# Graph attention, two layers: the last norm of a row block taken in smaller lots, and the last sweep closed tile by tile

## Chip, cores and metric
One core of one Trainium2 chip runs the whole program. The metric is the device time of an execution in microseconds (us); lower is better.

## What is computed
Two layers of graph attention over N = 4096 nodes with 256 features, each followed by a residual and a layer norm. Cut to what matters:

```python
# layer 1; layer 0 is alike with 8 heads of 128, an elu and a projection
xt  = einsum('ni,hio->hno', x, W)                 # 4 heads of 64
e   = leaky_relu(src[:, :, None] + dst[:, None, :], 0.2)
e   = where(adj > 0, e, -inf)
h   = einsum('hij,hjf->hif', softmax(e, axis=2), xt)
x   = layernorm(x + h.transpose(1, 0, 2).reshape(n, 256))
```

## The kernel before
Layer 0 takes the first 2255 us. Nothing in it is touched, except that two semaphores of GpSimd and SyncE become one.

Layer 1 runs in 16 sweeps `g`: four row blocks of 1024 rows, and in each the four heads. A sweep multiplies a 4096 x 1024 pattern by the head's values. The exponential of a sum is a product of exponentials on either side of the slope's kink, so the pattern is only zeros and ones, in two halves (`m` = 0 and 1), and the values come as high and low parts. A sweep has eight chunks `k` of 512 source rows. For a chunk ScalarE (and VectorE, for one of four rows of tiles in five of the eight chunks) compares thresholds (`compare2`, L1028 and L1422); VectorE masks the result with the adjacency and splits it (`split2`, L1433 and L1434); TensorE takes 64 matmuls (8 output tiles `t`, 4 source tiles, 2 halves) into eight PSUM banks, one for each output tile (`sweep2`, L835). Pattern buffers are four deep.

VectorE's order is written by hand. In sweep `g` it does the split of chunks 2 to 7 of `g` and of chunks 0 and 1 of `g + 1` (turns `m` = 0 to 7, L1577), each after the next turn's compare, and then takes the sums of `g` out of PSUM (`evacuate2`, L1443; ScalarE copies the first half, `copy_sums2`, L1042) and divides (`divide2`, L1451 to L1458, the last of them adds into `z`). So TensorE works on chunks 0 and 1 of the next sweep during that, and then waits for the split of chunk 2. TensorE may start a tile of the next sweep when VectorE has taken that tile's sums (`s_ev2`).

When the four heads of a row block are through, `z` holds x + h for its 1024 rows (eight tiles of 128 x 256). Its norm runs in the first sweep of the next block (g = 4, 8, 12): statistics of all eight tiles and their aggregation at turn 0 (`final_stats`, L1463, and `final_norm`, L1471 and L1473), a square root on ScalarE behind the compares of chunk 3 (`final_root`, L1046), a reciprocal at turn 2 (`final_scale`, L1478), and the scaling in two lots of four tiles at turns 3 and 4 (`final_apply`, L1483). SyncE's queue then stores `z` in one DMA, waits for it, and loads the next 1024 rows into it (L634, L636); the first head's `divide2` waits for that load (`s_zl`). Behind the last sweep the same steps run with nothing else left to do; there ScalarE scales four tiles (L1142) and VectorE the other four, and two DMAs store them (L651).

Of the kernel before, what the change touches and what calls it, by code (L numbers as in the profile page):

```python
# [17 lines left out]
P = 128  # L18
# [12 lines left out]
CPB = 8  # L31
# [56 lines left out]
def network(nc, x, adj, W, a1, a2, feat, W_out, b_out, Wn, c1, c2, x1, out):  # L88
# [28 lines left out]
    with ExitStack() as ctx:  # L117
# [64 lines left out]
        s_xm, s_pw, s_cw, s_mo = (s.sem(n) for n in ("xm", "pw", "cw", "mo"))  # L182
# [19 lines left out]
        CW2 = blk2 // 4  # L202
        G2, FIRST, WHOLE = H2 * NB2, H2, CPB - 2
# [54 lines left out]
        s_tn, s_rr, s_oh, s_ol = (s.sem(n) for n in ("tn", "rr", "oh", "ol"))  # L258
# [8 lines left out]
        s_zl, s_sd, s_sq, s_rs2, s_ap, s_o = (s.sem(n) for n in ("zl", "sd", "sq", "rs_", "ap", "o"))  # L267
        s_fin = [s.sem(f"fin_{p}") for p in range(2)]
# [77 lines left out]
        def _(pool):  # L346
# [45 lines left out]
            def ones2(c):  # L392
                pool.wait_ge(s_f2, c + 1)
                if c > 0:
                    pool.wait_ge(s_us, 16 * c)
                if c == CPB - 1:
                    pool.wait_ge(s_uv2[0][WHOLE], 16)
                nc.gpsimd.tensor_copy(stage_one(0), by_head(eu2, c))
                nc.gpsimd.tensor_copy(stage_one(2), by_head(ev2, c)).then_inc(s_oh, 1)
                pool.wait_ge(s_oh, c + 1)  # L400
                nc.gpsimd.tensor_tensor(stage_one(1), by_head(eu2, c), stage_one(0), ALU.subtract)
                nc.gpsimd.tensor_tensor(stage_one(3), by_head(ev2, c), stage_one(2), ALU.subtract).then_inc(s_ol, 1)
# [21 lines left out]
        def _(sp):  # L424
# [64 lines left out]
            def store_stage(c):  # L489
# [4 lines left out]
                sp.wait_ge(s_ol, c + 1)  # L494
# [13 lines left out]
            def tiles(dram, b):  # L508
                return dram.rearrange("(t p) f -> p t f", p=P)[:, b * TPB2:(b + 1) * TPB2, :]
# [107 lines left out]
            sp.dma_start(z[:, :, :], tiles(x1, 0)).then_inc(s_zl, 16)  # L617
# [31 lines left out]
            for p in range(2):  # L649
                sp.wait_ge(s_fin[p], 1)  # L650
                sp.dma_start(tiles(out, NB2 - 1)[:, p * TPB2 // 2:(p + 1) * TPB2 // 2, :],  # L651
                             z[:, p * TPB2 // 2:(p + 1) * TPB2 // 2, :]).then_inc(s_o, 16)
            sp.wait_ge(s_o, 16 * (NB2 + 1))

        @block.tensor
        def _(pe):
# [152 lines left out]
            def sweep2(g):  # L809
# [3 lines left out]
                for k in range(CPB):  # L813
# [29 lines left out]
                    last.then_inc(s_pe2, 1)  # L843

# [53 lines left out]
        def _(act):  # L898
# [148 lines left out]

            for n in range(16):
                copy_x(n)
# [73 lines left out]
            for g in range(G2):  # L1123
                if g > 0:
                    compare2(g, ahead2, range(lead, JC2))
                for k in range(ahead2 + 1 if g > 0 else CPB - 1, CPB):
                    compare2(g, k, range(JC2))
                    if g > 0 and g % H2 == 0 and k == ahead2 + 1:
                        final_root(g // H2 - 1)
# [5 lines left out]
                copy_sums2(g, 0)  # L1135
                if g + 1 < G2:
                    compare2(g + 1, ahead2, range(lead))
                copy_sums2(g, batch)
            final_root(NB2 - 1)
            act.wait_ge(s_n, 2 * NT + 2 * NB2 + 1)  # L1140
            for u in range(TPB2 // 2, TPB2):
                ins = act.activation(z[:, u, :], z[:, u, :], ACT.Identity, bias=mv[:, u, 1:2], scale=rs[:, u:u + 1])  # L1142
            ins.then_inc(s_fin[1], 1)

        @block.vector
        def _(dve):
# [289 lines left out]
            def evacuate2(g):  # L1436

                for t in range(TPB2):
                    if g == 0 and t == 0:
                        dve.wait_ge(s_sx, 1)  # L1440
                    if t % batch == 0:
                        dve.wait_ge(s_e2, TPB2 // batch * g + (t // batch + 1))
# [3 lines left out]
            def divide2(g):  # L1446

                h, b = g % H2, g // H2
                dve.wait_ge(s_ev2, TPB2 * (g + 1))
                ch = Chain(dve, s_dv2, 3 * g)  # L1450
                ch.link(dve.tensor_tensor(vt2, vt2, e2[:, :, V1:2 * V1], ALU.add))  # L1451
                ch.link(dve.reciprocal(zr2[:, :], vt2[:, :, D2:V1].rearrange("p t a -> p (t a)")))
                v = vt2[:, :, 0:D2]
                ch.link(dve.tensor_tensor(v, v, zr2[:, :].unsqueeze(2).to_broadcast([P, TPB2, D2]), ALU.mult))  # L1454
                if h == 0:
                    dve.wait_ge(s_zl, 16 * (b + 1))
                part = z[:, :, h * D2:(h + 1) * D2]
                dve.tensor_tensor(part, part, v, ALU.add).then_inc(s_dz, 1)  # L1458

            def final_stats(b, tiles):  # L1460
                dve.wait_ge(s_dz, H2 * (b + 1))
                for u in tiles:
                    last = dve.bn_stats(st[:, u, :], z[:, u, :])  # L1463
                last.then_inc(s_n, 1)

            def final_norm(b):
                at = 2 * NT + 2 * b
                dve.wait_ge(s_n, at + 1)
                ch = Chain(dve, s_n, at + 1)
                for u in range(TPB2):  # L1470
                    last = dve.bn_aggr(mv[:, u, :], st[:, u, :])  # L1471
                ch.link(last)
                dve.tensor_scalar(rt[:, :], mv[:, :, 1:2].rearrange("p u a -> p (u a)"), LN_EPS, None,  # L1473
                                  ALU.add).then_inc(s_sd, 1)

            def final_scale(b):
                dve.wait_ge(s_sq, b + 1)
                dve.reciprocal(rs[:, :], rt[:, :]).then_inc(s_rs2, 1)  # L1478

            def final_apply(b, tiles, signal):  # L1480
                dve.wait_ge(s_rs2, b + 1)
                for u in tiles:
                    last = dve.tensor_scalar(z[:, u, :], z[:, u, :], mv[:, u, 0:1], rs[:, u:u + 1], ALU.subtract,  # L1483
                                             ALU.mult)
                last.then_inc(signal, 1)
# [89 lines left out]
            for g in range(G2):  # L1575
                turns = [(g, k) for k in range(ahead2, CPB)] + ([(g + 1, k) for k in range(ahead2)] if g + 1 < G2 else [])
                for m, (gk, k) in enumerate(turns):  # L1577
# [30 lines left out]
                evacuate2(g)  # L1608
                divide2(g)
# [5 lines left out]
            final_stats(NB2 - 1, range(TPB2))  # L1615
            final_norm(NB2 - 1)
            final_scale(NB2 - 1)
            dve.wait_ge(s_rs2, NB2)
            dve.scalar_tensor_tensor(mv[:, :, 1:2].rearrange("p u a -> p (u a)"),
                                     mv[:, :, 0:1].rearrange("p u a -> p (u a)"), -1.0, rs[:, :],  # L1620
                                     ALU.mult, ALU.mult).then_inc(s_n, 1)
            final_apply(NB2 - 1, range(TPB2 // 2), s_fin[0])
# [26 lines left out]
```

## Time and profile before
| | |
|---|---|
| median of 3 runs | 2777.14 us (2777.05 to 2778.43) |
| the profiled execution | 2780.41 us, span 2778.7 us |
| TensorE busy | 2686.8 us, 97% |
| VectorE busy | 1982.1 us, 71% |
| ScalarE busy | 2064.3 us, 74% |
| granted TensorE clock | 0.991 on average |

Times in rows are microseconds from the start of the span. Engines: PE is TensorE, PEld its weight loads, DVE VectorE, ACT ScalarE, SPq the DMA queue that SyncE issues on. A row of a timeline has start, length, engine, line, operation, what it writes and reads, and how many instructions were merged; in brackets stands how long the engine was idle before it and what ended that.

### The profile page before, as it was taken

Reading aid. Unit: us, or ns where it says so; the run is one execution under the profiler, and the core shown is the slowest. Engines: PE = TensorE matmul, PEld = TensorE weight load, DVE = VectorE, ACT = ScalarE, POOL = GpSimd, SP = SyncE. Lnnn points to the kernel's source line nnn. Section 1 sums busy time; section 2 is a strip of 40 time slices with the busy share of each in tenths; the row PEclk is TensorE's granted clock in tenths of the full one; section 3 lists DMA queues with packets and bytes.
Section 4 is the critical chain, followed back from the end, with each engine's and each line's share of the span. In section 5 each row is a group of like instructions: output and inputs, shape, how many; then the busy total and the mean of one; then the engine's idle time right before and its main releaser. Section 6 shows DMA issues by size and latency. Waiting matters only on the chain.

```text
span 2778.7 us, 62377 instructions
## 1 busy us (share of the span) xinstructions
PE 2686.8 (97%) x26475; PEld 2327.5 (84%) x26475; DVE 1982.1 (71%) x3186; ACT 2064.3 (74%) x3216; POOL 563.7 (20%) x449
## 2 busy tenths in 40 slices
PE   7879999999999999999999999999999989999997
PEld 3438887888888888888888888888888879999997
DVE  5455669667776776777677677675655679988897
ACT  4447787677777777777777777777764579999996
POOL 0030018223231422323232142230002310000000
PEclk9999999999999999999999999999999999999999
DMA  7995431110110101111010111002115555323330
GB/s 248 392 328 178 152 114 45 30 34 22 42 30 23 40 26 30 37 31 30 20 43 27 27 37 34 26 21 56 34 46 166 185 194 190 109 79 121 105 109 17
DMA packets 192793, 241.57 MB, mean 87 GB/s; under 512 B 14074, under 2 KB 113658, under 8 KB 192508
## 3 DMA queue, kind: packets, MB, share of 16 engines
q1 hardware_dynamic: 192516, 237.59, 26.5%
q8 instruction: 209, 3.42, 0.5%
q14 instruction: 68, 0.56, 0.1%
HBM read 179.69 MB, written 57.05 MB: 85 GB/s over the span
## 4 chain that ended last, share of the span: by engine, by line
PE 73%; DVE 5%; ACT 4%; issue 1%; POOL 0%; DMA 0%; ACTq 0%; DVEq 0%
PE l_ps L726 57%; PE l_ps L835 9%; PE l_ps L763 4%; ACT l_arena L1028 3%; PE l_ps L788 1%; DVE l_arena L1434 1%; PE l_ps L751 1%; DVE l_arena L1433 1%; DVE l_arena L1443 1%; ACT l_arena L1042 0%; DVE l_arena L1463 0%; DVE l_arena L1422 0%; DVE l_arena L1451 0%; DVE l_arena L1454 0%; DVE l_arena L1458 0%
## 5 line engine op out<-in xcount | busy, mean ns | idle before, releaser
L726 PE MATMUL l_ps<-l_arena 128*128 128x258 f16 x16384 | 1834.8, 273 | 6.3 <-POOL l_arena L380 3.4
L726 PEld LDWEIGHTS l_ps<-l_arena 128*128 128x128 fp8e4 x16384 | 1592.8, 97 | 246.0 <-issue 3.7
L941 ACT ACTIVATE l_arena<-l_arena 128x512 fp8e4<-128x512 f32 x2048 | 1281.4, 708 | 89.2 <-PE l_ps L726 89.1
L1240 DVE SCALAR_TENSOR_TENSOR l_arena<-l_arena,l_mask 128x512 uint32<-128x512 uint32 x512 | 469.2, 916 | 408.4 <-ACT l_arena L941 405.6
L835 PE MATMUL l_ps<-l_arena 128*128 128x130 f16 x8192 | 487.6, 221 | 23.2 <-DVE l_arena L1434 13.3
L835 PEld LDWEIGHTS l_ps<-l_arena 128*128 128x128 fp8e4 x8192 | 482.5, 98 | 28.2 <-DVE l_arena L1434 22.9
L1241 DVE TENSOR_TENSOR l_arena<-l_arena,l_mask 128x512 uint32<-128x512 uint32 x512 | 490.2, 957 | 0.0
L1028 ACT ACTIVATE l_arena<-l_arena 128x1024 fp8e4<-128x1024 f32 x434 | 456.7, 1142 | 3.5 <-PE l_ps L835 3.4
L373 POOL TENSOR_TENSOR l_arena<-l_arena 128x516 f32<-128x516 f32 x120 | 156.8, 1306 | 1264.1 <-PE l_ps L726 1172.3
L959 ACT COPY l_arena<-l_ps 128x258 f32<-128x258 f32 x256 | 93.5, 368 | 245.2 <-PE l_ps L726 245.2
L1246 DVE SCALAR_TENSOR_TENSOR l_arena<-l_ps,l_arena 128x258 f32<-128x258 f32 x256 | 117.0, 482 | 147.9 <-ACT l_arena L959 147.9
L380 POOL TENSOR_TENSOR l_arena<-l_arena 128x516 f16<-128x516 f32 x120 | 176.5, 1488 | 32.5 <-DVE l_arena L1227 28.1
L1433 DVE SCALAR_TENSOR_TENSOR l_arena<-l_arena,l_mask 128x1024 uint32<-128x1024 uint32 x128 | 156.4, 1222 | 28.7 <-ACT l_arena L1028 27.8
L374 POOL TENSOR_TENSOR l_arena<-l_arena 128x516 f16<-128x516 f32 x120 | 174.4, 1453 | 0.0
L1434 DVE TENSOR_TENSOR l_arena<-l_arena,l_mask 128x1024 uint32<-128x1024 uint32 x128 | 156.1, 1219 | 0.0
L693 PE MATMUL l_ps<-l_mask 128*128 128x512 f32 x264 | 131.2, 637 | 0.0
L947 ACT ACTIVATE l_arena<-l_arena 128x512 f32<-128x512 f32 x64 | 40.6, 635 | 109.3 <-DVE l_arena L1272 109.3
L763 PE MATMUL l_ps<-l_arena 128*128 128x256 f32 x512 | 116.6, 381 | 0.0
L763 PEld LDWEIGHTS l_ps<-l_arena 128*128 128x128 f32 x512 | 95.8, 190 | 14.0 <-ACT l_arena L965 0.2
L913 ACT COPY l_arena<-l_ps 128x512 f32<-128x512 f32 x66 | 38.3, 582 | 90.6 <-DMA l_wh<-l_arena 67.5
L1202 DVE TENSOR_SCALAR l_arena<-l_arena 128x1024 fp8e4<-128x1024 int32 x52 | 40.0, 769 | 76.1 <-ACT l_arena L925 76.0
L693 PEld LDWEIGHTS l_ps<-l_mask 128*128 128x128 f32 x264 | 50.2, 203 | 48.7 <-issue 48.4
(152 smaller groups left out, 1208.8 us busy)
## 6 DMA issues: line engine op xcount, KB each, us to landing
l_arena<-in_adj SPq DMA_DIRECT2D x128, 512.0 KB, 6.5
l_arena<-uv SPq DMA_DIRECT2D x125, 260.0 KB, 5.7
l_wh<-l_arena SPq DMA_DIRECT2D x64, 256.0 KB, 9.5
l_arena<-l_srow SPq DMA_DIRECT2D x64, 256.0 KB, 3.2
l_arena<-l_wh SPq DMA_DIRECT2D x64, 256.0 KB, 4.7
feat<-l_arena SPq DMA_DIRECT2D x64, 256.0 KB, 2.2
l_arena<-feat SPq DMA_DIRECT2D x32, 512.0 KB, 3.6
uv<-l_arena SPq DMA_DIRECT2D x8, 1040.0 KB, 5.1
```

The source lines that it names most:

```text
L374: last = nc.gpsimd.tensor_tensor(part(h, c, j), whx[k][:, :, :], factor(f, h, c), ALU.mult)
L380: last = nc.gpsimd.tensor_tensor(part(h, c, j + 1), t[:, :, :], part(h, c, j), ALU.subtract)
L693: last = nc.tensor.matmul(banks[i % 3], rowsof, wall[:, k, q * H // 2:(q + 1) * H // 2, :], start=(k == 0), stop=(k == KF - 1))
L726: last = nc.tensor.matmul(sums(t, m), pattern(k, m).bitcast(F8)[:, j, t * P:(t + 1) * P], uv[:, slot(h, order[k]) + j, 2 * m * W1:2 * (m + ...
L763: last = nc.tensor.matmul(py[t % 2], ft[t % 2][:, k, :], wo[:, k, :], start=(k == 0), stop=(k == KO - 1))
L835: last = nc.tensor.matmul(sums2(t, m), pattern2(k, m).bitcast(F8)[:, j, t * P:(t + 1) * P], uv2[:, q, at:at + 2 * V1], start=(k == 0 and j ...
L941: ins = act.activation(pattern(k, 0).bitcast(F8)[:, j, :], s1b[q][:, :], ACT.Relu, bias=kc[:, h, jt:jt + 1], scale=STEEP, saturate=False)
L1028: ins = act.activation(pattern2(k, 0).bitcast(F8)[:, j, :], s1b2[:, q, :], ACT.Relu, bias=kc2[:, g % H2, jt:jt + 1], scale=STEEP, saturate ...
L1240: dve.scalar_tensor_tensor(c, v, ONE8X4, m, ALU.bitwise_xor, ALU.bitwise_and)
L1241: dve.tensor_tensor(v, v, m, ALU.bitwise_and).then_inc(s_bc, 1)
L1433: dve.scalar_tensor_tensor(c, v, ONE8X4, m, ALU.bitwise_xor, ALU.bitwise_and)
L1434: dve.tensor_tensor(v, v, m, ALU.bitwise_and).then_inc(s_bc2, 1)
```

## The change
- At a block's end (g = 4, 8, 12): statistics of tiles 0 to 3 at turn 0, of tiles 4 to 7 and the aggregation at turn 1; ScalarE's root after the compares of chunk 6 instead of chunk 3; the reciprocal at turn 4; scaling of tiles 0 to 2, 3 to 5, 6 and 7 at turns 4, 5 and 6.
- SyncE stores `z` and loads its next rows in three parts (`parts2`: tiles 0 to 2, 3 to 5, 6 and 7), each load after the store of the same part, in place of one DMA each way. The first load of `z` is three DMAs too.
- In the last sweep TensorE does chunks 0 to 4 as before, then waits for all patterns of the last three chunks and goes through them tile by tile (`CLOSE` is 3), so that a tile's sums are complete every 24 matmuls.
- Behind it everything goes in four pairs of tiles: ScalarE copies a pair's sums, VectorE evacuates, divides and takes the pair's statistics, ScalarE takes the root, VectorE makes the factors (`last_shift`), ScalarE alone scales, and SyncE stores 256 KB.
- `evacuate2` waits before each tile instead of before each fourth.

```diff
@@ SyncE, block end
-                    sp.wait_ge(s_ap, 2 * (g // H2))
-                    sp.dma_start(tiles(out, g // H2 - 1), z[:, :, :]).then_inc(s_o, 16)
-                    sp.wait_ge(s_o, 16 * (g // H2))
-                    sp.dma_start(z[:, :, :], tiles(x1, g // H2)).then_inc(s_zl, 16)
+                    b = g // H2 - 1
+                    for p, (first, last) in enumerate(parts2):
+                        sp.wait_ge(s_ap, 3 * b + p + 1)
+                        sp.dma_start(tiles(out, b, first, last), z[:, first:last, :]).then_inc(s_o[p], 16)
+                        if p > 0:
+                            sp.wait_ge(s_o[p - 1], 16 * (b + 1))
+                            load_z(b + 1, *parts2[p - 1])
+                    sp.wait_ge(s_o[2], 16 * (b + 1))
+                    load_z(b + 1, *parts2[2])
@@ TensorE, last sweep
-                for k in range(CPB):
+                for k in range(CPB - CLOSE if g == G2 - 1 else CPB):
...
+                if g == G2 - 1:
+                    pe.wait_ge(s_bc2, CPB * G2)
+                    for t in range(TPB2):
+                        for k in range(CPB - CLOSE, CPB):
+                            for j in range(JC2):
+                                ...
+                        if t < TPB2 - 1:
+                            last.then_inc(s_mm2, 1)
+                    last.then_inc(s_pe2, CLOSE)
@@ ScalarE
-                    if g > 0 and g % H2 == 0 and k == ahead2 + 1:
+                    if g > 0 and g % H2 == 0 and k == CPB - 2:
                         final_root(g // H2 - 1)
...
+            last_sums(0)
+            last_sums(1)
+            for p in range(4):
+                last_root(p)
+                if p < 2:
+                    last_sums(p + 2)
+                last_apply(p)
@@ VectorE, block end
-                        if m == 0:
-                            final_stats(g // H2 - 1, range(TPB2))
-                            final_norm(g // H2 - 1)
-                        if m == 2:
-                            final_scale(g // H2 - 1)
-                        if m in (3, 4):
-                            final_apply(g // H2 - 1, range(4 * (m - 3), 4 * (m - 2)), s_ap)
+                        if m < 2:
+                            final_stats(HALF * m, HALF * (m + 1), g)
+                        if m == 1:
+                            final_norm(0, TPB2, 2 * NT + 3 * b + 2)
+                        if m == 4:
+                            final_scale(0, TPB2, b + 1)
+                        if 4 <= m < 7:
+                            final_apply(b, *parts2[m - 4])
@@ VectorE, behind the last sweep
+            for p, (first, last) in enumerate(pairs2):
+                evacuate2(G2 - 1, first, last, lambda t: TPB2 // batch * (G2 - 1) + t // 2 + 1)
+                divide2(G2 - 1, first, last, 3 * (G2 - 1 + p))
+                if p > 0:
+                    last_shift(p - 1)
+                final_stats(first, last, G2 + p)
+                final_norm(first, last, base + 3 * p + 1)
+            last_shift(len(pairs2) - 1)
```

## Rows read from the trace of the kernel before
**Rows 1.** The page, part 4: the chain that ended last, by line of code.
```profile
PE l_ps L726 57%; PE l_ps L835 9%; PE l_ps L763 4%; ACT l_arena L1028 3%; PE l_ps L788 1%; DVE l_arena L1434 1%; PE l_ps L751 1%; DVE l_arena L1433 1%; DVE l_arena L1443 1%; ACT l_arena L1042 0%; DVE l_arena L1463 0%; DVE l_arena L1422 0%; DVE l_arena L1451 0%; DVE l_arena L1454 0%; DVE l_arena L1458 0%
```

**Rows 2.** Timeline of TensorE, last sweeps: start, length, instructions, idle before, releaser.
```profile
2518.91 3.91 PE L835 MATMUL l_ps<-l_arena 128*128 128x130 f16 x64 [0.36 <-DVE l_arena L1434]
2525.33 20.21 PE L835 MATMUL l_ps<-l_arena 128*128 128x130 f16 x320 [2.52 <-DVE l_arena L1434]
2546.26 37.66 PE L835 MATMUL l_ps<-l_arena 128*128 128x130 f16 x640 [0.71 <-DVE l_arena L1443]
2584.28 30.20 PE L835 MATMUL l_ps<-l_arena 128*128 128x130 f16 x512 [0.36 <-DVE l_arena L1434]
...
2672.74 37.64 PE L835 MATMUL l_ps<-l_arena 128*128 128x130 f16 x640 [2.07 <-DVE l_arena L1443]
...
2741.30 22.59 PE L835 MATMUL l_ps<-l_arena 128*128 128x130 f16 x384 [0.36 <-DVE l_arena L1434]
```

**Rows 3.** Timeline of VectorE and ScalarE in the ninth sweep, same columns.
```profile
2518.76 2.71 DVE L1463 BATCH_NORM_STATS2 l_arena<-l_arena 128x6 f32<-128x256 f32 x8
...
2522.38 0.21 ACT L1046 ACTIVATE l_arena<-l_arena 128x8 f32<-128x8 f32 x1 [4.86 <-DVE l_arena L1473]
2522.50 20.88 ACT L1028 ACTIVATE l_arena<-l_arena 128x1024 fp8e4<-128x1024 f32 x20
...
2525.81 1.23 DVE L1433 SCALAR_TENSOR_TENSOR l_arena<-l_arena,l_mask 128x1024 uint32<-128x1024 uint32 x1 [0.54 <-ACT l_arena L1028]
2526.96 1.22 DVE L1434 TENSOR_TENSOR l_arena<-l_arena,l_mask 128x1024 uint32<-128x1024 uint32 x1
...
2529.90 1.22 DVE L1433 SCALAR_TENSOR_TENSOR l_arena<-l_arena,l_mask 128x1024 uint32<-128x1024 uint32 x1 [1.00 <-ACT l_arena L1028]
...
2543.49 1.23 DVE L1433 SCALAR_TENSOR_TENSOR l_arena<-l_arena,l_mask 128x1024 uint32<-128x1024 uint32 x1 [0.50 <-ACT l_arena L1028]
...
2545.76 2.33 DVE L1443 SCALAR_TENSOR_TENSOR l_arena<-l_ps,l_arena 128x130 f32<-128x130 f32 x8
```

**Rows 4.** DMA issues of the whole run: count, KB each, median us to landing.
```profile
l_arena<-uv SPq DMA_DIRECT2D x125, 260.0 KB, 5.7
...
l_arena<-in_x SPq DMA_DIRECT2D x32, 128.0 KB, 2.3
x<-l_arena SPq DMA_DIRECT2D x32, 128.0 KB, 1.7
l_arena<-x SPq DMA_DIRECT2D x4, 1024.0 KB, 5.5
out<-l_arena SPq DMA_DIRECT2D x3, 1024.0 KB, 4.9
```

**Rows 5.** Two stretches by window; PEclk is the granted TensorE clock.
```profile
2525.30:2528.00 2.70, 2.67 (x25) 2.67 (x26) 2.19 (x2) 2.70 (x4) 0.00 (x0) 0.50 0.00 0
...
2651.80:2656.00 4.20, 4.20 (x72) 4.20 (x73) 3.09 (x4) 4.20 (x5) 0.00 (x0) 1.00 0.01 4
```

**Rows 6.** Timeline of the last 25 us, columns as in rows 2.
```profile
2754.68 1.22 DVE L1434 TENSOR_TENSOR l_arena<-l_arena,l_mask 128x1024 uint32<-128x1024 uint32 x1
...
2763.99 0.59 ACT L1042 COPY l_arena<-l_ps 128x520 f32<-128x520 f32 x1 [1.27 <-PE l_ps L835]
...
2772.51 2.07 ACT L1142 ACTIVATE l_arena<-l_arena 128x256 f32<-128x256 f32 x4 [0.47 <-DVE l_arena L1619]
2773.79 1.20 SPq L651 DMA_DIRECT2D out<-l_arena  x2
```

**Rows 7.** Groups of layer 1 by line and shape: busy us, mean ns.
```profile
L1422 DVE TENSOR_SCALAR l_arena<-l_arena 128x1024 fp8e4<-128x1024 f32 x78 | 60.0, 770 | 8.9 <-PE l_ps L835 8.9
...
L1451 DVE TENSOR_TENSOR l_arena<-l_arena 128x520 f32<-128x520 f32 x16 | 11.2, 700 | 0.5
...
L1046 ACT ACT_TABLE_LOAD x1 | 1.3, 1283 | 0.0
...
L1381 DVE TENSOR_TENSOR l_arena<-l_arena 128x24 f32<-128x24 f32 x1 | 0.2, 182 | 0.0
```

More of the change, by code:

```diff
@@ L506, in store_rows, with tiles, load_z @@
                     sp.dma_start(srow2[:, at:at + P], rows2[c % 2][t * H2:(t + 1) * H2, :]).then_inc(s_ro2[c % 2], 16)
-            def tiles(dram, b):
-                return dram.rearrange("(t p) f -> p t f", p=P)[:, b * TPB2:(b + 1) * TPB2, :]
+            def tiles(dram, b, first, last):
+                return dram.rearrange("(t p) f -> p t f", p=P)[:, b * TPB2 + first:b * TPB2 + last, :]
+            def load_z(b, first, last):
+                sp.dma_start(z[:, first:last, :], tiles(x1, b, first, last)).then_inc(s_zl, 16)
             def load_next():
@@ L616, in _ @@
             sp.wait_ge(s_xp, NT)
-            sp.dma_start(z[:, :, :], tiles(x1, 0)).then_inc(s_zl, 16)
+            for first, last in parts2:
+                load_z(0, first, last)
             store_rows(CPB - 2)
@@ L648, in _ @@
                             store_back(g + 1, n if g % 2 else WHOLE - 1 - n)
[L649 to L653, printed above, removed]
+            for p, (first, last) in enumerate(pairs2):
+                sp.wait_ge(s_fin, p + 1)
+                sp.dma_start(tiles(out, NB2 - 1, first, last), z[:, first:last, :]).then_inc(s_o[0], 16)
+            sp.wait_ge(s_o[0], 16 * (NB2 - 1 + len(pairs2)))
         @block.tensor
@@ L1443, in evacuate2, with divide2 @@
                     dve.scalar_tensor_tensor(e2[:, t, :], sums2(t, 1), sc2[:, g % H2, g // H2 * TPB2 + t:g // H2 * TPB2 + t + 1],
                                              e2[:, t, :], ALU.mult, ALU.add).then_inc(s_ev2, 1)
-            def divide2(g):
+            def divide2(g, first, last, base):
                 h, b = g % H2, g // H2
[L1449 to L1454, printed above, removed]
-                if h == 0:
-                    dve.wait_ge(s_zl, 16 * (b + 1))
-                part = z[:, :, h * D2:(h + 1) * D2]
-                dve.tensor_tensor(part, part, v, ALU.add).then_inc(s_dz, 1)
@@ L1460, in final_stats @@
[L1460 to L1473, printed above, removed]
+                dve.wait_ge(s_ev2, TPB2 * g + last)
@@ new lines, in divide2 @@
+                ch = Chain(dve, s_dv2, base)
+                part = vt2[:, first:last, :]
+                inverse = zr2[:, first:last]
+                ch.link(dve.tensor_tensor(part, part, e2[:, first:last, V1:2 * V1], ALU.add))
+                ch.link(dve.reciprocal(inverse, part[:, :, D2:V1].rearrange("p t a -> p (t a)")))
+                v = part[:, :, 0:D2]
+                ch.link(dve.tensor_tensor(v, v, inverse.unsqueeze(2).to_broadcast([P, last - first, D2]), ALU.mult))
+                if h == 0:
+                    dve.wait_ge(s_zl, 48 * (b + 1))
@@ new lines, in divide2, with final_stats, final_norm @@
+                into = z[:, first:last, h * D2:(h + 1) * D2]
+                dve.tensor_tensor(into, into, v, ALU.add).then_inc(s_dz, 1)
+            def final_stats(first, last, ready):
+                dve.wait_ge(s_dz, ready)
+                for u in range(first, last):
+                    ins = dve.bn_stats(st[:, u, :], z[:, u, :])
+                ins.then_inc(s_n, 1)
+            def final_norm(first, last, base):
+                dve.wait_ge(s_n, base)
+                ch = Chain(dve, s_n, base)
+                for u in range(first, last):
+                    ins = dve.bn_aggr(mv[:, u, :], st[:, u, :])
+                ch.link(ins)
+                dve.tensor_scalar(rt[:, first:last], mv[:, first:last, 1:2].rearrange("p u a -> p (u a)"), LN_EPS, None,
@@ L1474, in final_norm, with final_scale, final_apply @@
                                   ALU.add).then_inc(s_sd, 1)
[L1476 to L1480, printed above, removed]
+            def final_scale(first, last, count):
+                dve.wait_ge(s_sq, count)
+                dve.reciprocal(rs[:, first:last], rt[:, first:last]).then_inc(s_rs2, 1)
+            def final_apply(b, first, last):
                 dve.wait_ge(s_rs2, b + 1)
[L1482 to L1485, printed above, removed]
+                for u in range(first, last):
+                    ins = dve.tensor_scalar(z[:, u, :], z[:, u, :], mv[:, u, 0:1], rs[:, u:u + 1], ALU.subtract, ALU.mult)
+                ins.then_inc(s_ap, 1)
```

83 lines of the change are left out of this document (55 added, 28 removed).

## Prediction

> **What bounds the kernel.** I read the page's chain first. TensorE holds most of it, and layer 1's matmuls (L835) are 9% of the span [rows 1]. So a microsecond counts only where TensorE waits, or behind its last matmul. The timeline of TensorE alone shows where that is. In a plain sweep 512 matmuls take 30.20 us and 0.36 us is idle, so from one start of chunk 2 to the next are 30.56 us [rows 2]. Around a block's end it is different: from 2518.91 to 2584.28, two sweeps, are 65.37 us against 61.12, so a block's end costs 4.25 us. The trace has three, each with a wait of 2.51 or 2.52 us before chunk 3 and another before the next sweep (0.71 in the one shown, 2.07 in the last [rows 2]).
>
> The timeline of VectorE and ScalarE says who causes it. VectorE's statistics sit between the split of chunk 2 and of chunk 3; ScalarE stands at its root for 4.86 us until they are through; and since its compares are then late, VectorE itself idles 0.54, 1.00 and 0.50 us before three later splits [rows 3]. TensorE's next sweep starts 0.50 us after VectorE begins to take the sums (2545.76 to 2546.26 [rows 2, 3]). So VectorE's row of work, and not TensorE's 30 us, sets the length of this sweep.
>
> Last I read the end of the timeline. Three chunks at 3.75 us (37.66 us hold ten and 0.16 of pipeline [rows 2]) after 2741.30 end chunk 4 at 2752.6. The last split ends at 2755.9. TensorE ends at 2763.89; 14.8 us follow.
>
> **Block's end, added up.** Zero is 2518.76, the start of the statistics. Costs from start to start: an instruction behind another starts 0.08 to 0.09 us before the end of the one ahead (1.23 long, 1.15 apart), so a split is 2.27 [rows 3], a compare, 0.77 long [rows 7], takes 0.66 to 0.68, and a statistic 0.33 (2.71 for eight [rows 3]).
> - Turn 0: four statistics 1.31, compare 0.66, split of chunk 3 2.27: 4.24. TensorE needs 0.14 from a split's end to its start; it starts chunk 3 at 4.38 instead of 3.90, a wait near 0.5.
> - Turn 1: four statistics with their wait 1.43, aggregation and epsilon. The old row of eight statistics to epsilon takes 3.50, from 2518.76 to 2522.26, of which 2.74 are statistics; 0.76 is left. The split of chunk 4 ends at 8.70; TensorE wanted it at 8.13, a second wait of 0.7.
> - Turns 2 to 4: two compares, two splits 14.56; reciprocal with its wait 0.24; three tiles at 0.32 (four L1483 take 1.29) 15.77.
> - Turns 5 to 7: three splits, one compare, five tiles: 24.86.
>
> Before, the same mark, the first L1443, lies at 27.00. The three idles from start to start come to 2.25 (2.04 shown, and some 0.07 of lost overlap at each); 27.00 - 2.25 + 0.11 for the second lot's and the factor's waits gives 24.86 again. Does a new idle come in? ScalarE's compares are 1.044 apart (20 in 20.88 [rows 3]). Without the stop at the root it has chunk 4 at 1.9, 5 at 6.0, 6 at 9.2, 7 at 12.4, the next sweep's 0 and 1 at 17.0 and 20.1; VectorE wants them at 6.4, 9.4, 12.3, 15.8, 19.7 and 22.6. The least room is 2.5 us. The table load before the first root, 1.28 once [rows 7] and so far hidden behind ScalarE's stop, fits. TensorE has finished the sweep at 23.8 and starts the next at 25.36 instead of 27.50. From there all is as before. **Gain 2.14 us at each of three ends: 6.4 us.** The cost of work isn't less; what goes are idles. Bounds: 0 if other idles take their place, 2.25 if the second lot's wait is free.
>
> **Reload of z.** The last scaling ends at 22.7 instead of 19.0, the add needs `z` at 28.9. From 128 KB in 1.7 and 1024 KB in 4.9 a store is 3.6 ns for a KB and 1.25 fixed; loads (2.3 and 5.5) are 1.85 fixed [rows 4]. The last part, 256 KB, is stored by 24.9 and loaded by 27.7; the longer parts went before. Room 1.2 us, so I take 0. The issues behind it on SyncE's queue (a row load and eight of the values) start some 1.5 us later and are wanted 30 us later. The first load as three DMAs delays that queue by two issues, 0.8 us, at the start of layer 1; Taken as 0, at most 0.8.
>
> **Per-tile waits.** Three more waits a sweep lie on the path. Eight evacuations take 2.33 us with a wait in the middle that ended late [rows 3]; waits already met have no row of their own. Between 0 and 0.03 us each (the gap that a true chain shows): 0 to 1.4 us over 15 sweeps. I take 0, since the wait can be read while the 0.35 us instruction ahead runs.
>
> **The close.** TensorE now needs the last split before the first of three chunks. It ends at 2755.8 [rows 6], so matmuls start at 2755.95 instead of 2752.6: 3.3 us late, for sure. A pair of tiles is 48 matmuls, 2.82 us.
> VectorE's pair: evacuation 0.66; add of 130 columns, reciprocal, product, add into `z`. Their price I take on the line between 24 columns in 0.182 and 520 in 0.700 [rows 7], 1.04 ns a column: 0.29 each, the reciprocal 0.17, with waits 1.13. Then the factors of the pair ahead 0.29, two statistics 0.77, aggregation 0.29, epsilon 0.08: **3.2 us**, against TensorE's 2.82. So VectorE sets the pace from the first pair on. Its first pair starts 3.48 after TensorE's start (2.98 and 0.1, as at 2763.99 [rows 6], and the copy of 260 columns, 0.4), at 2759.43; the fourth's epsilon ends 12.7 later, at 2772.1. ScalarE's root and the factors are 0.70, two tiles of scaling 1.08 (four take 2.07 [rows 6]): 2773.9. A 256 KB store lands in 2.2 and 0.4 closes the span: 2776.5. Against 2778.7 that is a gain of 2.2 us.
>
> **The clock.** After one wait of 2.52 us the granted clock was 0.50, the 1.2 GHz level; after another of 2.51 it was 1.00, 2.4 GHz [rows 5]. At 0.50 the 320 matmuls took 20.21 us instead of 18.9, 1.3 more; it cost nothing, as VectorE was later still. TensorE's wait before the close is 3.2 us and has nothing behind which to hide: each pair comes 1.3 later. I take the fall as likelier than not: **gain of the close 0.9 us** with it, 2.2 without.
> The Trainium skill, "TensorE: Matmul & The Clock Gate", section "Why this matters for your kernels", tells kernels to avoid gaps between bursts because the clock then falls back to its lower level. By that rule the sum is the 0.9; the trace agrees in some of its waits only.
>
> **Sum.** 6.4 + 0.9 = 7.3 us, made on the profiled span; 2780.41 of that execution lies 3.3 above the median, which shifts the level and not the difference. 2777.14 - 7.3 = **2769.8 us**.
>
> **Rivals.**
> - *Full clock in the close* (0.25): 2777.14 - 6.4 - 2.2 = 2768.5. For it: one of the three long waits at block ends left the clock up [rows 5].
> - *The block ends give only part* (0.17). The clock may now fall at the start of sweeps 5, 9 and 13, after a wait of 1.5 us, where TensorE has no room: up to 3 x 1.3 = 3.9 us, 2773.7. Against it: 640 matmuls after the wait of 2.07 took 37.64, no more than the 37.66 after 0.71 [rows 2]. Or idles of VectorE return by half: 3.2, 2773.0.
> - *The pairs don't pay* (0.10). Many short instructions for few: if a pair costs VectorE 3.7 instead of 3.2 (each small step 0.05 dearer), the end is 2.0 later and the close loses 1.1: 2771.8.
> - *Slower* (0.03). The reload of z comes late: four transfers share one queue at the same time. Transfers of 260 KB had a median of 5.7 us [rows 4]. If store and load of the last part each took that, `z` would be there at 34.1, 5.2 late, of which 0.25 is room: 3 x 4.9 = 14.8, 2784.6. It decides from a landing at 31.6. Against it: that median is of queues of eight; here one part waits for another's store.
>
> **How the numbers follow.** The forecast has 0.45. A measurement here can tell about 0.2%, 5.6 us, from no change. Below 2771.6 lie the forecast, the first rival and a bit of the others: faster 0.73; the rest of the partial cases: same 0.24; slower 0.03. Range 2767.2 (full clock, a pair of 3.0, 0.4 more at the end) to 2773.8 (next to all of the partial cases).
>
> **What the new profile must show.** Waits of 0.5 and 0.7 before chunks 3 and 4 in place of 2.5, and about 1.5 before sweeps 5, 9 and 13; two sweeps at a block's end in 63.2 us; VectorE never idle on ScalarE there, ScalarE no longer at the root; a wait of 3.2 before the close and perhaps a clock of 0.50; pairs 3.2 apart on VectorE; some 2.5 us from the last issue to the end. Wrong it would be if L1458's successor waited for a DMA, or if sweeps 5, 9, 13 ran at the lower clock.

## The result and the profile after

| | before | changed |
|---|---|---|
| median | 2777.97 us (17 runs) | 2771.68 us (17 runs) |
| ratio | | 0.9975, 95% interval 0.9969 to 0.9982 |
| profiled execution, span | 2778.7 us | 2769.8 us |

The kernel became 0.25% faster, 6.3 us by the medians; 7.3 were forecast. The two profiled spans differ by 8.9 us, more than that, and the trace says where. Layer 0, where only two semaphores became one, was 3.7 us shorter in this execution (layer 1's first matmul is at 2251.61 and was at 2255.35), and sweeps 0 to 3 were 1.4 longer. About 1.0 of the 1.4 is sweep 1, whose 512 matmuls took 31.25 us instead of 30.21; the granted clock was 0.50 in its first 2.7 us. What the change touches is 5.3 us at the block ends and 1.3 us in the close: 5.3 + 1.3 + 3.7 - 1.4 = 8.9. So I compare stretches of the profiled executions, one for each run, and not spans: two sweeps from the start of chunk 2 at a block's end to the start of chunk 2 two sweeps on, and the last sweep's chunk 2 to the end of the span.

TensorE's timeline in the changed kernel, with the same columns as [rows 2]. L846 are the sweeps, L865 is the close:

```profile
2514.43 3.91 PE L846 MATMUL l_ps<-l_arena 128*128 128x130 f16 x64 [0.36 <-DVE l_arena L1485]
2518.66 3.91 PE L846 MATMUL l_ps<-l_arena 128*128 128x130 f16 x64 [0.33 <-DVE l_arena L1485]
2523.13 15.12 PE L846 MATMUL l_ps<-l_arena 128*128 128x130 f16 x256 [0.56 <-DVE l_arena L1485]
2539.65 37.92 PE L846 MATMUL l_ps<-l_arena 128*128 128x130 f16 x640 [1.39 <-DVE l_arena L1493]
2577.93 30.20 PE L846 MATMUL l_ps<-l_arena 128*128 128x130 f16 x512 [0.37 <-DVE l_arena L1485]
...
2664.26 7.64 PE L846 MATMUL l_ps<-l_arena 128*128 128x130 f16 x128 [1.40 <-DVE l_arena L1493]
2672.55 30.19 PE L846 MATMUL l_ps<-l_arena 128*128 128x130 f16 x512 [0.66 <-DVE l_arena L1485]
...
2733.66 11.38 PE L846 MATMUL l_ps<-l_arena 128*128 128x130 f16 x192 [0.36 <-DVE l_arena L1485]
2748.32 12.64 PE L865 MATMUL l_ps<-l_arena 128*128 128x130 f16 x192 [3.28 <-DVE l_arena L1485]
```

At the ninth sweep the wait of 2.52 us is gone. In its place are 0.33, 0.56 and, before the next sweep, 1.39 (0.48, 0.72 and 1.52 more than a plain chunk, from start to start). The two sweeps from 2514.43 to 2577.93 take 63.50 us; before they took 65.37 [rows 2]. The three block ends take 63.23, 63.50 and 64.07. The last is the dearest, and one more wait shows in it, 0.66 us in front of chunk 2 at 2672.55.

VectorE, ScalarE and SyncE's queue in the same sweep (L1515 statistics, L1075 root, L1493 evacuation, L1510 the add into `z`, L643 and L515 store and load of `z`, L479 and L485 loads of rows and values):

```profile
2514.29 1.40 DVE L1515 BATCH_NORM_STATS2 l_arena<-l_arena 128x6 f32<-128x256 f32 x4
...
2518.53 1.40 DVE L1515 BATCH_NORM_STATS2 l_arena<-l_arena 128x6 f32<-128x256 f32 x4
...
2523.34 0.20 ACT L1075 ACTIVATE l_arena<-l_arena 128x8 f32<-128x8 f32 x1
...
2536.99 0.37 SPq L643 DMA_DIRECT2D out<-l_arena  x1
2537.41 2.18 SPq L515 DMA_DIRECT2D l_arena<-x  x2
...
2539.16 2.16 DVE L1493 SCALAR_TENSOR_TENSOR l_arena<-l_ps,l_arena 128x130 f32<-128x130 f32 x8
...
2539.69 0.41 SPq L479 DMA_DIRECT2D l_arena<-srow  x1
2540.14 5.49 SPq L485 DMA_DIRECT2D l_arena<-uv  x8
...
2543.69 0.69 DVE L1510 TENSOR_TENSOR l_arena<-l_arena 128x512 f32<-128x512 f32 x1 [0.67 <-DMA l_arena<-x]
```

The root no longer has an idle ahead of it (4.86 us in [rows 3]). From the first statistic to the first evacuation are 2539.16 - 2514.29 = 24.87 us, where it was 27.00. The last row is new: VectorE waits 0.67 us for the load of `z`. In the last block end the same wait is 1.24 us.

The close: copies of a pair's sums on ScalarE, the first evacuation of each pair on VectorE, the last scaling on ScalarE:

```profile
2752.65 0.38 ACT L1083 COPY l_arena<-l_ps 128x260 f32<-128x260 f32 x1 [6.85 <-PE l_ps L865]
2753.06 0.61 DVE L1493 SCALAR_TENSOR_TENSOR l_arena<-l_ps,l_arena 128x130 f32<-128x130 f32 x2 [4.79 <-ACT l_arena L1083]
...
2756.04 0.60 DVE L1493 SCALAR_TENSOR_TENSOR l_arena<-l_ps,l_arena 128x130 f32<-128x130 f32 x2
...
2759.15 0.61 DVE L1493 SCALAR_TENSOR_TENSOR l_arena<-l_ps,l_arena 128x130 f32<-128x130 f32 x2
...
2762.27 0.61 DVE L1493 SCALAR_TENSOR_TENSOR l_arena<-l_ps,l_arena 128x130 f32<-128x130 f32 x2
...
2766.14 1.09 ACT L1093 ACTIVATE l_arena<-l_arena 128x256 f32<-128x256 f32 x2 [0.43 <-DVE l_arena L1541]
```

The evacuations start 2.98, 3.11 and 3.12 us apart. TensorE's matmuls started at 2748.32 behind a wait of 3.28 us. In windows at its start (PEclk is the third number from the right):

```profile
2748.30:2751.00 2.70, 2.68 (x25) 2.68 (x26) 0.00 (x0) 0.00 (x0) 0.00 (x0) 0.50 0.00 0
2751.00:2755.00 4.00, 4.00 (x70) 4.00 (x69) 1.77 (x7) 0.38 (x1) 0.00 (x0) 0.99 0.02 4
```

The clock was granted at 0.50, the 1.2 GHz level, for the first 2.7 us, with 25 matmuls in them; after that 70 fit into 4.0 us. The 192 take 12.64 us and not 11.4.

### The profile page after: what moved, and what is told of

Same layout as the page of the kernel before. It is cut to its first block, busy times and chain, and to the rows that moved or that the text cites. A ratio compares the mean times of both kernels' runs of the same rounds, so it can differ in the third digit from the quotient of the medians.

```text
span 2769.8 us, 62417 instructions
## 1 busy us (share of the span) xinstructions
PE 2681.0 (97%) x26475; PEld 2322.7 (84%) x26475; DVE 1982.7 (72%) x3203; ACT 2068.0 (75%) x3225; POOL 563.8 (20%) x449
## 4 chain that ended last, share of the span: by engine, by line
PE 73%; DVE 6%; ACT 2%; issue 1%; DMA 0%; POOL 0%; ACTq 0%; DVEq 0%
PE l_ps L737 57%; PE l_ps L846 9%; PE l_ps L774 4%; ACT l_arena L1057 2%; DVE l_arena L1485 1%; DVE l_arena L1484 1%; PE l_ps L799 1%; PE l_ps L762 1%; DVE l_arena L1473 1%; DVE l_arena L1493 1%; ACT l_arena L1071 0%; DVE l_arena L1515 0%; DVE l_arena L1510 0%; DMA l_arena<-x 0%; DVE l_arena L1503 0%
## 5 line engine op out<-in xcount | busy, mean ns | idle before, releaser
L846 PE MATMUL l_ps<-l_arena 128*128 128x130 f16 x8000 | 476.1, 220 | 19.6 <-DVE l_arena L1485 9.5
L846 PEld LDWEIGHTS l_ps<-l_arena 128*128 128x128 fp8e4 x8000 | 470.3, 98 | 25.3 <-DVE l_arena L1485 20.7
```

The source lines that it names most:

```text
L846: last = nc.tensor.matmul(sums2(t, m), pattern2(k, m).bitcast(F8)[:, j, t * P:(t + 1) * P], uv2[:, q, at:at + 2 * V1], start=(k == 0 and j ...
```

## Experiments

All compare stretches as above; "ends" are the three pairs of sweeps and "close" is chunk 2 of the last sweep to the end. The kernel before has 65.37, 65.37, 65.37 and 37.4. A ratio is taken to runs of the kernel before on the same chip; their medians are 2778.01 (e1 to e4), 2779.11 (e5 to e8) and 2778.86 us (e9 to e12).

| run | ends, us | close, us | median, us | ratio to before, 95% |
|---|---|---|---|---|
| changed | 63.23, 63.50, 64.07 | 36.1 | 2771.68 | 0.9975 (0.9969 to 0.9982) |
| e1 close only | 65.38, 65.37, 65.36 | 36.5 | 2776.19 | 0.9994 (0.9986 to 1.0003) |
| e2 block ends only | 63.24, 63.42, 63.22 | 37.4 | 2771.34 | 0.9973 (0.9965 to 0.9982) |
| e3 statistics in one lot | 65.37, 65.29, 65.26 | 34.9 | 2775.06 | 0.9990 (0.9981 to 0.9999) |
| e4 root early | 68.30, 68.45, 68.29 | 36.1 | 2786.15 | 1.0029 (1.0018 to 1.0039) |
| e5 queue waits for z | 63.23, 63.24, 63.50 | 36.3 | 2768.48 | 0.9967 (0.9954 to 0.9979) |
| e6 scaling a turn earlier | 63.24, 63.24, 63.25 | 36.5 | 2768.88 | 0.9966 (0.9954 to 0.9978) |
| e7 close of two chunks | 63.24, 63.46, 64.06 | 34.3 | 2768.30 | 0.9964 (0.9951 to 0.9976) |
| e8 both | 63.24, 63.24, 63.24 | 34.2 | 2767.38 | 0.9958 (0.9946 to 0.9971) |
| e9 one transfer | 66.65, 68.41, 68.50 | 36.2 | 2784.59 | 1.0024 (1.0015 to 1.0033) |
| e10 close of one chunk | 63.23, 63.65, 63.72 | 37.0 | 2771.39 | 0.9974 (0.9965 to 0.9983) |
| e11 changed, again | 63.22, 63.51, 63.50 | 34.8 | 2772.57 | 0.9978 (0.9969 to 0.9987) |
| e12 both, again | 63.23, 63.22, 63.23 | 34.3 | 2768.54 | 0.9964 (0.9951 to 0.9978) |

Medians and stretches agree only roughly. For e5 the medians give 10.6 us and the stretches 7.2; for e11 they give 6.3 and 8.5. Only the profiled execution of each run has a trace; what the others did in layer 0, at the ends and in the close is not known.

### e1 and e2: each half of the change alone

e1 keeps the block ends of before (root behind chunk 3, reciprocal at turn 2, two lots of scaling, one DMA each way):

```diff
-                        if m < 2:
-                            final_stats(HALF * m, HALF * (m + 1), g)
-                        if m == 1:
+                        if m == 0:
+                            final_stats(0, HALF, g)
+                            final_stats(HALF, TPB2, g)
                             final_norm(...)
-                        if m == 4:
+                        if m == 2:
                             final_scale(...)
-                        if 4 <= m < 7:
-                            final_apply(b, *parts2[m - 4])
+                        if m in (3, 4):
+                            final_apply(b, 4 * (m - 3), 4 * (m - 2))
```

> Only the close of the last sweep is changed; at the three block ends statistics, root, scaling and the one store and load of z stand as before. Theory (two separate gains): two sweeps at a block end stay at 65.4 us; from the last sweep's chunk 2 to the end of the span 36.1 to 36.2 us against 37.4 before, with the clock at 0.50 at the close's start, so the kernel is 1.3 us faster than before. Rival (the close pays nothing, the changed kernel's gain is all from the block ends): 37.4 us again, no change in time.

e2 keeps the last sweep of before:

```diff
-                for k in range(CPB - CLOSE if g == G2 - 1 else CPB):
+                for k in range(CPB):
...
-            for p, (first, last) in enumerate(pairs2):
-                ...
+            final_stats(0, TPB2, G2)
+            final_norm(0, TPB2, base + 1)
+            final_scale(0, TPB2, NB2)
```

> Only the block ends are changed; the last sweep and what follows it are as before. Theory: two sweeps at the three ends take 63.2, 63.5 and 64.1 us (65.4 before), give or take 0.4 for the landing of z, so 5.3 us faster than before, and 37.4 us from the last chunk 2 to the end. Rival (the close brings more than its own 1.3 us, since the sweeps' clock or transfers act on each other): less than 4 us faster.

The two gains stand apart, as both theories had it, with two stretches off their numbers: e1's close is 36.5 us where 36.1 to 36.2 were expected, and e2's third end is 63.22 where 64.1 was. TensorE in e1 (L841 sweeps, L860 close):

```profile
2519.98 20.17 PE L841 MATMUL l_ps<-l_arena 128*128 128x130 f16 x320 [2.52 <-DVE l_arena L1480]
2540.91 37.65 PE L841 MATMUL l_ps<-l_arena 128*128 128x130 f16 x640 [0.76 <-DVE l_arena L1488]
...
2750.59 12.96 PE L860 MATMUL l_ps<-l_arena 128*128 128x130 f16 x192 [3.28 <-DVE l_arena L1480]
```

The wait of 2.52 at the block's end and the 3.28 before the close stand side by side. e1's close is 0.9 us shorter than before, and the interval of its ratio includes 1: by the times the close alone can't be told from nothing. e2 has 6.2 us less in its three ends (2.13 + 1.95 + 2.15) and is 0.27% faster. So what the measurement sees is the block ends.

### e3: statistics in one lot, root late

```diff
-                        if m < 2:
-                            final_stats(HALF * m, HALF * (m + 1), g)
-                        if m == 1:
+                        if m == 0:
+                            final_stats(0, HALF, g)
+                            final_stats(HALF, TPB2, g)
                             final_norm(...)
```

> The changed kernel with the statistics of all eight tiles at turn 0 again; the late root and the late scaling in three lots stay. Theory (what goes is VectorE's idling behind ScalarE's early root): TensorE waits 2.5 us before chunk 3 as in the kernel before, yet the first evacuation still starts 24.8 us after the statistics and two sweeps take 63.2 to 64.1 us; time that of the changed kernel. Rival (what goes is TensorE's wait of 2.5 us before chunk 3, by the two lots): two sweeps go back to 65.4 us, 5 to 6 us slower than the changed kernel.

My theory missed here, and the rival's number came out: 65.3 us. TensorE, and at the end of the ninth sweep ScalarE's copy of the sums:

```profile
2518.50 3.91 PE L846 MATMUL l_ps<-l_arena 128*128 128x130 f16 x64 [0.36 <-DVE l_arena L1485]
2524.92 27.96 PE L846 MATMUL l_ps<-l_arena 128*128 128x130 f16 x448 [2.51 <-DVE l_arena L1485]
2543.50 0.59 ACT L1071 COPY l_arena<-l_ps 128x520 f32<-128x520 f32 x1 [2.01 <-PE l_ps L846]
2553.24 30.19 PE L846 MATMUL l_ps<-l_arena 128*128 128x130 f16 x512 [0.36 <-DVE l_arena L1485]
2583.79 30.20 PE L846 MATMUL l_ps<-l_arena 128*128 128x130 f16 x512 [0.36 <-DVE l_arena L1485]
...
2740.71 11.38 PE L846 MATMUL l_ps<-l_arena 128*128 128x130 f16 x192 [0.36 <-DVE l_arena L1485]
2755.36 11.39 PE L865 MATMUL l_ps<-l_arena 128*128 128x130 f16 x192 [3.27 <-DVE l_arena L1485]
```

The 448 matmuls behind the wait take 27.96 us. At 3.75 us a chunk, and 0.16, they should take 26.4. The windows say what held them (and, second, that in this execution the clock did not fall in the close):

```profile
2524.90:2528.00 3.10, 3.08 (x29) 3.08 (x30) 3.10 (x4) 2.71 (x4) 0.00 (x0) 0.50 0.00 0
...
2755.30:2758.00 2.70, 2.64 (x46) 2.65 (x47) 0.00 (x1) 0.00 (x0) 0.00 (x0) 1.00 0.00 0
```

At all three ends the granted clock was 0.50 or 0.52 behind the wait. So there are two rows of work of about the same length at a block's end. VectorE's is 27.0 us to the first evacuation in the kernel before and 24.9 in the changed one. TensorE's is the wait of 2.5, its 30 us, and 1.5 us of lower clock. Before, the fall was hidden behind VectorE: the third end, where the clock stayed up [rows 5], took 65.37 as well. With the late root VectorE is out of the way (the copy waits 2.01 us for TensorE, and TensorE does not wait before the next sweep), and TensorE's own row sets 65.3. The late root alone buys 0.1 us in this execution. Without the fall it would be about 65.3 - 1.5 = 63.8 us an end, an estimate from these rows. The profiled execution, 2777.71 us, is among the slowest of e3's eleven (2771.07 to 2777.94), so in others the clock may have stayed up; no trace shows them.

### e4: statistics in two lots, root early

```diff
-                    if g > 0 and g % H2 == 0 and k == CPB - 2:
+                    if g > 0 and g % H2 == 0 and k == ahead2 + 1:
                         final_root(g // H2 - 1)
```

> The changed kernel with ScalarE's root behind the compares of chunk 3 again; the statistics stay in two lots. Theory: ScalarE stands some 7.7 us until the epsilon at turn 1, VectorE idles 3.3, 1.2 and 0.2 us behind it, the first evacuation starts 29.8 us after the statistics, two sweeps take 68 us, 8 us more than before over three ends, 12 to 14 us slower than the changed kernel. Rival (the two lots alone make the gain): 63.2 to 64.1 us, time of the changed kernel.

As the theory had it: VectorE waits for ScalarE's compares up to 3.5 us, and TensorE for VectorE.

```profile
DVE l_arena L1484 <- ACT l_arena L1057: 29.1, 36, 3.5
```

```profile
2525.49 3.91 PE L846 MATMUL l_ps<-l_arena 128*128 128x130 f16 x64 [0.33 <-DVE l_arena L1485]
2533.52 17.39 PE L846 MATMUL l_ps<-l_arena 128*128 128x130 f16 x256 [4.12 <-DVE l_arena L1485]
```

68.3 to 68.5 us at each end, 3 us more than before. The two lots with the early root are worse than nothing. Each half of the reordering needs the other: the lots keep TensorE's waits short, so that the clock stays up, the late root keeps ScalarE going, and together they give 2.1 us.

### e5 and e6: the late load of z

e5 holds the row load and the eight value loads back until `z` has landed:

```diff
+                if g > 0 and g % H2 == 0:
+                    sp.wait_ge(s_zl, 48 * (g // H2 + 1))
                 if g < G2 - 2:
                     sp.wait_ge(s_ca2, CPB * (g + 1))
```

> The changed kernel, but at a block end SyncE waits for all three loads of z before it issues the row load and the eight loads of the values. Theory (the last part of z lands late because those nine transfers share the 16 DMA engines with it): VectorE's wait for z (0.67 and 1.24 us in two of the changed kernel's three block ends) is gone, the last part lands 2.8 us after its issue instead of 4.5 to 5.0, and two sweeps take 63.2 to 63.3 us at all three. Rival (the last part is late by itself, behind its own store and the second part's load): waits of 0.5 to 1.2 us stay and one pair of sweeps is at 64 us again.

SyncE's queue in e5 at the ninth sweep (two loads of `z`, then the row load behind the wait), and VectorE's wait for `z` in all three ends:

```profile
2540.44 2.15 SPq L515 DMA_DIRECT2D l_arena<-x  x2
...
2545.28 0.33 SPq L479 DMA_DIRECT2D l_arena<-srow  x1
```

```profile
DVE l_arena L1512 <- DMA l_arena<-x: 0.7, 1, 0.7
```

The second load is issued near 2542.2 and the queue goes on at 2545.28, 3.1 us later; in the changed kernel the same load took 4.4. Two of the three ends are at 63.23 and 63.24. But one wait of 0.7 stayed: there the load took 4.4 us with nothing behind it in the queue. And the changed kernel's first end has the nine transfers right behind the load too, which landed soon all the same:

```profile
L515 SPq DMA_DIRECT2D l_arena<-x x1: 367/367/367, 2414.8 to 2414.8; - x1
DMA to landing us min/median/max: 3.1/3.1/3.1
```

Landings of the last part, in us, at the three ends:

| | first | second | third |
|---|---|---|---|
| changed, e2, e7, e10 and e11: nine behind | 3.1 to 3.9 | 4.3 to 4.6 | 4.1 to 5.0 |
| e5: none behind | 3.0 | 3.0 | 4.4 |
| e6, e8 and e12: nine behind, a turn earlier | 2.7 to 2.8 | 2.8 to 4.5 | 2.8 to 4.4 |

So the theory holds at the second end and the rival at the third. Nine transfers behind a load do not make it late by themselves, as its landings after 2.7 and 2.8 us in e6 show; what else does stays open.

The Trainium skill, "DMA: Bandwidth & Descriptors", section "Issuing engines are not separate DMA queues", says that transfers share the same 16 DMA engines and interleave. The second end agrees, with 3.0 us against 4.3 to 4.6; the third does not show it.

e6 makes `z` ready earlier, with the root behind chunk 5:

```diff
-                    if g > 0 and g % H2 == 0 and k == CPB - 2:
+                    if g > 0 and g % H2 == 0 and k == CPB - 3:
                         final_root(g // H2 - 1)
...
-                        if m == 4:
+                        if m == 3:
                             final_scale(0, TPB2, b + 1)
-                        if 4 <= m < 7:
-                            final_apply(b, *parts2[m - 4])
+                        if 3 <= m < 6:
+                            final_apply(b, *parts2[m - 3])
```

> The changed kernel with the root behind the compares of chunk 5 and the reciprocal and scaling one turn earlier (turns 3, 4, 5). Theory: VectorE's work is the same, so the first evacuation still starts 24.9 us after the statistics; the last scaling ends 2.9 us earlier, z is there in time, and two sweeps take 63.2 us at all three block ends, 1 us faster than the changed kernel. Rival (ScalarE's root now comes too near to the epsilon and ScalarE's compares are late again): VectorE idles behind ScalarE in these sweeps and they take 64 us or more.

```profile
2512.24 3.91 PE L846 MATMUL l_ps<-l_arena 128*128 128x130 f16 x64 [0.37 <-DVE l_arena L1485]
...
2575.48 30.20 PE L846 MATMUL l_ps<-l_arena 128*128 128x130 f16 x512 [0.36 <-DVE l_arena L1485]
...
2636.59 3.91 PE L846 MATMUL l_ps<-l_arena 128*128 128x130 f16 x64 [0.36 <-DVE l_arena L1485]
...
2699.84 30.20 PE L846 MATMUL l_ps<-l_arena 128*128 128x130 f16 x512 [0.36 <-DVE l_arena L1485]
```

2575.48 - 2512.24 and 2699.84 - 2636.59 are 63.24 and 63.25 us, and VectorE's waits for `z` are gone: even a load of 4.0 us is in time here, and in e8 one of 4.5. That is the number of the forecast for a block's end with nothing late.

### e7 and e10: how many chunks to close tile by tile

```diff
-        HALF, CLOSE = TPB2 // 2, 3
+        HALF, CLOSE = TPB2 // 2, 2        # e10: 1
```

> The changed kernel with CLOSE = 2: only the last two chunks are gone through tile by tile. Theory (the close with three chunks pays its gain back by a wait of 3.3 us for the last split and by the clock that falls in it): no wait before the close, clock at 1.00, VectorE's first pair starts 17.6 us after chunk 2's start instead of 19.4, from chunk 2 to the end 34.3 us instead of 36.1, 1.8 us faster than the changed kernel. Rival (the earlier first pair is of no use, since the last pair waits for TensorE or for ScalarE): 35.5 us or more.

TensorE in e7, then VectorE's first evacuation in e7 and in e10:

```profile
2736.03 15.12 PE L846 MATMUL l_ps<-l_arena 128*128 128x130 f16 x256 [0.36 <-DVE l_arena L1485]
2750.98 7.63 PE L865 MATMUL l_ps<-l_arena 128*128 128x130 f16 x128
```

```profile
2753.51 0.61 DVE L1493 SCALAR_TENSOR_TENSOR l_arena<-l_ps,l_arena 128x130 f32<-128x130 f32 x2 [2.89 <-ACT l_arena L1083]
```

```profile
2754.55 0.61 DVE L1493 SCALAR_TENSOR_TENSOR l_arena<-l_ps,l_arena 128x130 f32<-128x130 f32 x2 [5.70 <-ACT l_arena L1083]
```

In e7 the row of the close (L865) has no wait before it, since the last split is just done, and the 128 matmuls take 7.63 us at full clock. VectorE's first pair starts 17.5 us after chunk 2, and the end comes 34.3 us after it, on the number.

> The changed kernel with CLOSE = 1: only the last chunk tile by tile, as in the kernel before, with the pairs behind it. Theory (VectorE's four pairs of 3.1 us set the end, so only the time of the first pair counts): its first pair starts 20.4 us after chunk 2's start (19.4 with three chunks, 17.6 with two), 37.1 us from chunk 2 to the end. Rival (with the pairs the order of the chunks is of no matter, TensorE just has to end early): TensorE ends as early as with two, so 34.3 us.

In e10 the first pair starts 20.3 us after chunk 2 (its stretch begins at 2734.26) and the close is 37.0 us. TensorE ends 22.6 us after chunk 2 (27.3 with three chunks), and it doesn't help. What counts is when the first pair can start, as VectorE then needs its four pairs whatever TensorE does.

### e9: z in one transfer

```diff
-                    for p, (first, last) in enumerate(parts2):
-                        ...
+                    sp.wait_ge(s_ap, 3 * (b + 1))
+                    sp.dma_start(tiles(out, b, 0, TPB2), z[:, 0:TPB2, :]).then_inc(s_o[0], 16)
+                    sp.wait_ge(s_o[0], 16 * (b + 1))
+                    load_z(b + 1, 0, TPB2)
```

> The changed kernel, but z is stored and loaded at a block end in one DMA each way behind the third lot of scaling. Theory (the late scaling is only possible with the parts): last scaling ends 22.7 us after the statistics, store and load of 1 MB take 5 and 5.5, z lands at 33.2 to 34.0, VectorE waits 4.3 to 5.1 us for it at each end, two sweeps take 67 to 68 us, 12 to 14 us slower than the changed kernel. Rival (the transfer is hidden anyway): 63.2 to 64.1 us.

VectorE's waits for `z` over the three ends, and TensorE behind them at the first and second end:

```profile
DVE l_arena L1505 <- DMA l_arena<-x: 12.0, 3, 4.1
2425.33 30.19 PE L841 MATMUL l_ps<-l_arena 128*128 128x130 f16 x512 [3.25 <-DVE l_arena L1480]
2553.29 31.74 PE L841 MATMUL l_ps<-l_arena 128*128 128x130 f16 x512 [3.45 <-DVE l_arena L1480]
```

12.0 us, 4 each. Two of the pairs of sweeps took 68.4 and 68.5, more than the 67 to 68 expected: behind waits of 3.45 and 3.52 us the granted clock was 0.50 and 0.52, and 512 matmuls took 31.7 to 31.8 us. At the first end, behind 3.25, it stayed at 1.00. With the late scaling, a single store and load make the change a loss of 0.24%. The parts on SyncE's queue are no ornament; they are what makes the late scaling pay.

### e8, e11 and e12: the two repairs together, beside the changed kernel

e8 and e12 have e6's edit and e7's.

> Both at once: CLOSE = 2, root behind chunk 5 and scaling at turns 3 to 5. Theory: 63.2 us at all three block ends and 34.3 us from the last chunk 2 to the end, 9.5 us faster than the kernel before and 2 to 3 us faster than the changed one. Rival (the parts share a limit): no more than either alone.

> The changed kernel itself, on the same chip as the next one. Theory: two sweeps 63.2 to 64.1 us, close 36.1 us when the clock is at 0.50 in its first 2.7 us and 34.9 us when it is not.

> CLOSE = 2, root behind chunk 5, scaling at turns 3 to 5, again beside the changed kernel. Theory: 63.2 us and 34.3 us as before, 2.2 to 3 us faster than the changed kernel on the same chip.

Both stretches came out twice: 63.2 us three times, 34.2 and 34.3. By the medians of one chip e12 is 2768.54 and the changed kernel 2772.57, 4.0 us apart, though the ratios' intervals overlap (0.9964, 0.9951 to 0.9978, and 0.9978, 0.9969 to 0.9987). The two traces show 1.1 us of it: 0.55 at the ends and 0.55 in the close, since e11's close ran at full clock. Against the first profile of the changed kernel, whose close did not, e8's stretches are 3.0 us shorter. Against the kernel before the stretches give 6.4 + 3.2 = 9.6 us, and 9.5 were expected; the medians beside it on the same chips were 11.7 (2779.11 to 2767.38) and 10.3 us higher. So this version has the shortest stretches of those tried. It is faster than the kernel before beyond doubt, and faster than the changed one by the traces. The medians of e5 to e8 lie within 1.5 us and don't rank these four.

## Why the prediction was right

**The block's end.** The step "24.86" for the first evacuation was 24.87. The row of VectorE's work, added up instruction by instruction, was right, and so were the waits of TensorE: 0.48, 0.72 and 1.52 from start to start, where 0.5, 0.7 and 1.5 were given. Where nothing was late the two sweeps took 63.23 us, and 63.2 was forecast.

**A statement that was too strong.** "VectorE's row of work, and not TensorE's 30 us, sets the length of this sweep" is true of the kernel before, but only half of it. e3 shows that TensorE's row with a 2.5 us wait and the fall of the clock behind it is as long (65.3; about 63.8 without the fall). The working counted only idles of VectorE as gain and would have given the same 2.1 us to the late root alone, which in e3's trace gives 0.1. The sum was right because the change also made the lots.

**The reload of z.** "Room 1.2 us, so I take 0" was the term that was mis-sized. The store of the last part took the 2.2 us that were given. The load was given 2.8 us and took 3.1, 4.4 and 5.0. The step missed that the transfers behind can share in the delay (e5's second end) and that a load varies by itself (its third). Where it was late, the add into `z` started 29.4 and 30.0 us after the statistics, 0.7 and 1.2 us late. Some 0.4 of each was room before TensorE (0.25 had been given), so the stretches lost 0.27 and 0.84 us, 1.1 of 6.4 us. The rival "slower" was the same mechanism with other numbers; what it lacked was only size. e9 shows at full size what a late `z` costs.

**The close.** The pair was given 3.2 us and took 3.1. The wait before the close was given as 3.2 and was 3.28. At full clock VectorE's first pair was forecast 2759.43 - 2741.30 = 18.13 us after chunk 2, and in e11 it started after 18.13 (2754.61 - 2736.48). The gain was given as 0.9 us with the clock at 0.50 and 2.2 without. It was 0.9 to 1.3 in the six closes with the lower clock (36.1 to 36.5) and 2.5 to 2.6 in the two without (34.9 in e3, 34.8 in e11). Both states occur: of the eight profiled executions that close with three chunks, six show the lower clock and two don't. So the first rival was no rival but the other face of the forecast. The Trainium skill, "TensorE: Matmul & The Clock Gate", section "Part 1: The HAM clock gate (the "warmup" mystery)", says that the same kernel can meet the gate differently from run to run. Here e11 and the changed kernel, the same code, agree with that: 34.8 and 36.1 us.

**Two terms that were rivals or zero.** The clock did not fall behind the waits of 1.4 us before sweeps 5, 9 and 13: after the first end 640 matmuls took 37.65 us, as before. The first load of `z` in three DMAs was taken as 0, at most 0.8. Sweeps 0 to 3 took 137.6 us on average in the eleven profiled executions that have it (136.8 to 138.5) and 137.0 in the three that don't. So this term is neither shown nor excluded.

**Waits before each tile** cost nothing that shows: a plain sweep takes 30.55 us from one chunk 2 to the next (2703.11 to 2733.66), as before, and the eight evacuations in a row take 2.16 us.

**The sum.** 5.3 and 1.3 us in the profiled stretches, 6.6, where 6.4 and 0.9 were given. The medians say 6.3. That these come so near is partly luck: the late reload took 1.1 us from the ends, and the close gave 0.4 more than its term. The forecast time, 2769.8 us, is 1.9 below the measured 2771.68; 0.8 of that is the median before, 2777.14 then and 2777.97 now. Both gains are shown in stretches of the trace; the medians alone could not have told them from each other.

## What to carry to other kernels

- Add up each engine's row between two marks, and look at the second longest too. Here VectorE's row gave 65.4 us and TensorE's 65.3, of which 1.5 was lower clock. In their traces either half of the change alone gave 0.1 us or lost 3 us an end.
- A step that is moved later takes its transfers with it. Leave a load room for its spread, and not only its usual time: the last part of `z`, 256 KB, landed after 2.6 to 5.0 us in 33 cases. Moving it one turn earlier (e6) paid where holding back the queue behind it (e5) helped at one end only.
- In a tail that is worked off in pieces by one engine, the start of the first piece counts. Closing more chunks tile by tile brings that start forward only until TensorE has to wait for the inputs of all of them: two chunks here, not three. Even at full clock three took 34.8 to 34.9 us and two 34.2 to 34.3.

## What was not expected of the hardware

- In e3 the granted clock was at 0.50 to 0.52 after all three waits of 2.5 us, in the kernel before and in e1 after two of three, and in the close it fell after six of eight waits of 3.3 us. Each of these falls cost TensorE 1.2 to 1.6 us. After e4's three waits of 4.1 us the cost was 2.1 to 2.3.
- A load of 256 KB took 3.0 us twice and 4.4 once with nothing behind it on its queue, and 2.6 to 5.0 us with nine transfers issued right behind it.
- Layer 1's first matmul, behind the almost untouched layer 0, started anywhere from 2250.1 to 2255.5 us in these profiled executions. That is nearly the size of the whole change.
